# Rank-one attention on one Trainium2 core: argument products over 32 rows, selections built a stage earlier, last averages moved behind the stage boundary

## The reference

```python
def _L3_conv_ref(x, g_w, g_b, theta_w, theta_b, phi_w, phi_b, W_w, W_b, bn_gamma, ...):
    x_avg = jnp.mean(x, axis=(2, 3), keepdims=True)
    se_mid = jax.nn.relu(conv1x1(x_avg, se1_w, se1_b))
    W_cw = jax.nn.sigmoid(conv1x1(se_mid, se2_w, se2_b))
    g_x = conv1x1(x, g_w, g_b).reshape(b, N)
    theta_x = conv1x1(x, theta_w, theta_b).reshape(b, N)
    phi_x = conv1x1(x, phi_w, phi_b).reshape(b, N)
    f = theta_x[:, :, None] * phi_x[:, None, :]
    f_div_C = jax.nn.softmax(f, axis=-1)
    y = jnp.einsum('bij,bj->bi', f_div_C, g_x)
    W_y = conv1x1(y, W_w, W_b)
    W_y = (W_y - bn_mean) * inv + bn_beta
    return W_cw * W_y + x
```

## Time and profile before

| | |
|---|---|
| time, median of 3 runs | 2866.69 us (2864.36 to 2867.64) |
| time of the profiled execution | 2868.04 us |
| its span in the trace | 2866.2 us |
| PE busy | 2743.7 us (96%) |
| DVE busy | 2156.5 us (75%) |
| ACT busy | 1663.3 us (58%) |
| POOL busy | 74.1 us (3%) |
| mean granted PE clock | 0.976 |

### The profile page before, as it was taken

The page is one execution under the profiler, slowest core; times in us unless marked ns, Lnnn a source line. Parts: engine busy times, 40 slices in busy tenths (PEclk is TensorE's granted clock), DMA queues, the critical chain, the costliest instruction groups (busy, mean ns, idle before and its releaser), DMA issues. The chain is left out here.

```text
span 2866.2 us, 45891 instructions
## 1 busy us (share of the span) xinstructions
PE 2743.7 (96%) x20113; PEld 1361.1 (47%) x20113; DVE 2156.5 (75%) x1392; ACT 1663.3 (58%) x2577; POOL 74.1 (3%) x66
## 2 busy tenths in 40 slices
PE   7399999999999999999999999999799999999898
PEld 3334444444344344443444444444478888757552
DVE  5499999999999999999999999998442221224344
ACT  2467776777777777777677777766422222211253
POOL 0000000000000000000000000000431000000000
PEclk9799999999999999999999999999899999999997
DMA  1100000000001000000000000100600000200001
GB/s 69 39 25 22 23 29 9 29 29 16 29 9 35 23 15 29 22 23 29 9 29 29 16 29 10 35 5 1 194 1 0 1 1 0 84 0 1 0 1 59
DMA packets 38760, 72.26 MB, mean 25 GB/s; under 512 B 21088, under 2 KB 22048, under 8 KB 36896
## 3 DMA queue, kind: packets, MB, share of 16 engines
q1 hardware_dynamic: 38496, 69.19, 7.4%
q0 software_dynamic: 64, 0.13, 0.0%
HBM read 60.45 MB, written 8.86 MB: 24 GB/s over the span
## 5 line engine op out<-in xcount | busy, mean ns | idle before, releaser
L734 PE MATMUL l_ps<-mlp_w,W2H 128*64 128x512 f16 x8192 | 1366.4, 392 | 18.0 <-DVE mlp_w L768 18.0
L768 DVE TENSOR_TENSOR mlp_w<-words_x,words_y 128x2048 f32<-128x2048 f32 x512 | 1159.5, 2287 | 66.9 <-PE l_ps L734 66.9
L734 PE MATMUL l_ps<-mlp_w,W2L 128*64 128x512 f16 x4096 | 802.3, 388 | 0.0
L734 PEld LDWEIGHTS l_ps<-mlp_w,W2H 128*64 128x64 f16 x8192 | 455.1, 108 | 550.1 <-issue 116.4
L815 ACT ACTIVATE relu_bottom<-l_ps 128x512 f32<-128x512 f32 x1024 | 612.3, 598 | 79.4 <-PE l_ps L734 1.4
L815 ACT ACTIVATE mlp_w<-l_ps 128x512 f32<-128x512 f32 x684 | 408.8, 598 | 279.7 <-PE l_ps L734 249.8
L752 DVE SCALAR_TENSOR_TENSOR mlp_w<-relu_bottom,sign_ratio,mlp_w 128x2048 f32<-128x2048 f32 x171 | 401.4, 2348 | 7.6 <-ACT relu_bottom L815 7.6
L734 PEld LDWEIGHTS l_ps<-mlp_w,W2L 128*64 128x64 f16 x4096 | 229.0, 109 | 179.7 <-issue 0.8
L815 ACT ACTIVATE relu_top<-l_ps 128x512 f32<-128x512 f32 x340 | 203.2, 598 | 135.7 <-PE l_ps L734 120.8
L723 PE MATMUL l_ps<-y_rows,y_weights_halves 12*128 12x512 bf16 x2048 | 202.4, 385 | 12.5 <-DMA y_rows<-y_pieces 12.5
L752 DVE SCALAR_TENSOR_TENSOR relu_top<-relu_bottom,sign_ratio,relu_top 128x2048 f32<-128x2048 f32 x85 | 199.5, 2348 | 4.0 <-ACT relu_bottom L815 4.0
(11 more groups left out here) (375 smaller groups left out, 2549.3 us busy)
## 6 DMA issues: line engine op xcount, KB each, us to landing
table_pos<-pos_table SPq DMA_DIRECT2D x64, 512.0 KB, 3.8
mlp_w<-in_mlp_w SPq DMA_DIRECT2D x8, 1024.0 KB, 13.2
X<-in_x SPq DMA_DIRECT2D x8, 512.0 KB, 7.4
bias_scratch<-bias_rows SPq DMA_DIRECT2D x64, 64.0 KB, 2.0
mlp_w_hi<-bias_scratch SPq DMA_DIRECT2D x16, 256.0 KB, 3.9
out<-Q SPq DMA_DIRECT2D x16, 256.0 KB, 2.1
y_rows<-y_pieces SPq DMA_DIRECT2D x192, 12.0 KB
xn_b<-in_out_wT SPq DMA_DIRECT2D x1, 1024.0 KB, 7.9
```

Source lines behind the costliest of these rows:

```text
L734: last = nc.tensor.matmul(out[q][a * DH:(a + 1) * DH, :], w[:, half], h[a][:, :, k], start=False, stop=stop, tile_position=(0, a * DH))
L768: nc.vector.tensor_tensor(hw[i % 3][:, r].rearrange("p (m j) -> p m j", j=J), words_x, words_y[:, 2 * n + r].unsqueeze(1).to_broadcast([P, ...
```

## The change

1. `gw`, `sel_q`, `sel_k`, `sel_m` become tiles of the stage before, and POOL's block that fills them moves there, followed by a wait of POOL for its own work. PE's wait for `sel` and DVE's wait for the zeroed `gw` in the rank-one stage go.
2. An argument product takes all 32 rows of its row tile in place of the first 2. The 30 further rows hold zeros in both operands, so the result is the same.
3. `weigh` waits once for both exponentials of its round, ahead of its four products, in place of once per pair.
4. `columns(0)` and `replicate(0, 0)` stand ahead of the weighing of their round, and `replicate(0, 1)` ahead of the last weighing.
5. The last four averages (t = 1) move from the end of ACT's stream in the non-local stage to the head of its stream in the rank-one stage; DVE waits for them (`av_in`) before it adds the halves.

```diff
@@ stage_nonlocal @@
+    K.sel_q, K.sel_k, K.sel_m, K.gw = room([P, B, P]), room([P, B, P]), room([P, B * NT, P]), room([P, CC, 32])
...
+        @block.gpsimd
+        def _(pool):
+            nc.gpsimd.memset(K.gw, 0.0).then_inc(sel, 1)
+            nc.gpsimd.memset(K.sel_q, 0.0).then_inc(sel, 1)
+            nc.gpsimd.memset(K.sel_k, 0.0).then_inc(sel, 1)
+            pool.wait_ge(sel, 3)
...
+            pool.wait_ge(sel, 3 + 4 * B * NT)
...
-            for i in range(NT * CC):
-                t, c = divmod(i, CC)
-                act.wait_ge(o_out, (B - 1) * NT * CC + i + 1)
-                act.wait_ge(mean, CC + i)
-                nc.scalar.activation(ex[2][:, 0:BANK], K.X[:, c, B - 1, t * BANK:(t + 1) * BANK], ACT.Copy,
-                                     accum_out=(K.av_b[:, c:c + 1] if t else K.av[:, c, 1:2])).then_inc(mean, 1)
+            for c in range(CC):
+                act.wait_ge(o_out, (B - 1) * NT * CC + c + 1)
+                act.wait_ge(mean, CC + c)
+                nc.scalar.activation(ex[2][:, 0:BANK], K.X[:, c, B - 1, 0:BANK], ACT.Copy, accum_out=K.av[:, c, 1:2]).then_inc(mean, 1)
@@ stage_rank_one @@
-            pe.wait_ge(sel, 3 + 4 * B * NT)
...
-                        last = nc.tensor.matmul(args[k % 3][:, u], keys[b][at:at + 2, jj * P:(jj + 1) * P], queries[b][at:at + 2, :],
+                        last = nc.tensor.matmul(args[k % 3][:, u], keys[b][at:at + 32, jj * P:(jj + 1) * P], queries[b][at:at + 32, :],
                                                 start=True, stop=True, tile_position=(at, 0))
...
+                pe.wait_ge(ex, NT * (r + 1))
                 for t in range(NT):
                     k = NT * r + t
-                    pe.wait_ge(ex, k + 1)
...
             for r in range(B * JJ):
                 arguments(r)
-                if r:
-                    weigh(r - 1)
                 if r == JJ + 1:
                     columns(0)
                 if r == JJ + 2:
                     replicate(0, 0)
+                if r:
+                    weigh(r - 1)
+            replicate(0, 1)
             weigh(B * JJ - 1)
-            replicate(0, 1)
             columns(1)
...
-            dve.wait_ge(sel, 1)
             nc.vector.tensor_copy(gw[:, :, 0:3], K.v("gtp_w", 0, 3 * CC).rearrange("p (c k) -> p c k", k=3)).then_inc(w_pad, 1)
+            dve.wait_ge(av_in, CC)
             nc.vector.tensor_tensor(av[:, :, 1], av[:, :, 1], K.av_b[:], ALU.add).then_inc(head, 1)
...
+            for c in range(CC):
+                if c:
+                    act.wait_ge(av_in, c)
+                nc.scalar.activation(scaled[1], K.X[:, c, B - 1, BANK:], ACT.Copy, accum_out=K.av_b[:, c:c + 1]).then_inc(av_in, 1)
             act.wait_ge(head, 3)
             act.wait_ge(g_mm, 1)
```

More of the change, by code:

```diff
@@ L1415, in stage_nonlocal @@
     z_mm, z_out, o_mm, o_out = K.sem("z_mm"), K.sem("z_out"), K.sem("nlo_mm"), K.sem("nlo_out")
-    bn, mean = K.sem("bn3_step"), K.sem("mean_sums")
+    bn, mean, sel = K.sem("bn3_step"), K.sem("mean_sums"), K.sem("selection")
     NF = 2 * B
@@ L1422, in stage_nonlocal @@
     with nc.Block() as block:
+        @block.gpsimd
[4 more added lines that the diff above has]
+            pool.wait_ge(sel, 3)
+            for b in range(B):
+                q, k = (w[:, b].rearrange("p (t u r) -> p t u r", t=NT, u=2) for w in (K.sel_q, K.sel_k))
+                for t in range(NT):
+                    n = 32 * (NT * b + t)
+                    nc.gpsimd.tensor_copy(q[:, t, :, 0:2], K.k("ident", n + 1, 1).unsqueeze(2).to_broadcast([P, 2, 2])).then_inc(sel, 1)
+                    nc.gpsimd.tensor_copy(k[:, :, t, 0], K.k("ident", n + 2, 1).to_broadcast([P, NT])).then_inc(sel, 1)
+                    nc.gpsimd.tensor_copy(k[:, :, t, 1], K.k("ident", 3, 1).to_broadcast([P, NT])).then_inc(sel, 1)
+            for n in range(B * NT):
+                nc.gpsimd.tensor_copy(K.sel_m[:, n], K.k("ident", 32 * n + 2, 1).to_broadcast([P, P])).then_inc(sel, 1)
+            pool.wait_ge(sel, 3 + 4 * B * NT)
         @block.tensor
@@ L1621, in stage_rank_one @@
     sums = [room([P, BANK]) for _ in range(B)]
-    sel_q, sel_k, sel_m = room([P, B, P]), room([P, B, P]), room([P, B * NT, P])
+    sel_q, sel_k, sel_m, gw = K.sel_q, K.sel_k, K.sel_m, K.gw
     out = carver(K.Q)([P, CC * B, HW])
-    gw = sb("gtp_w32", [P, CC, 32])
     mid, gate = sb("se_mid", [SE, B]), sb("gate", [P, CC, B])
@@ L1633, in stage_rank_one @@
     pps = args[1][:, 0, 0:2 * B * NT]
-    sel, w_pad, head = K.sem("selection"), K.sem("gtp_w_padded"), K.sem("r1_small")
+    w_pad, head, av_in = K.sem("gtp_w_padded"), K.sem("r1_small"), K.sem("avg_last")
     av_d, g_mm, g_out, t_mm, t_out = K.sem("avg_done"), K.sem("gtp_mm"), K.sem("gtp_out"), K.sem("rowsT_mm"), K.sem("rowsT_out")
@@ L1656, in _ @@
             sp.wait_ge(o_st, 16 * B * NT * CC)
[L1658 to L1672, removed]
         @block.tensor
```

## The result

| | before | changed |
|---|---|---|
| median, first comparison | 2865.53 us (4 runs, 2863.12 to 2867.64) | 2845.95 us (4 runs, 2845.16 to 2847.20) |
| ratio, 95% interval | | 0.9932 [0.9915, 0.9950] |
| profiled execution, span | 2868.04 us, 2866.2 | 2847.20 us, 2845.4 |
| mean granted PE clock | 0.976 | 0.983 |

The account below looks back on a forecast made before the run. PE, at half clock through 27.20 fully busy us of the rank-one loop, was taken as the bound. Handoff 1.0 us plus a shorter loop and tail made 15.4; 2866.69 - 15.4 = 2851.3 us, range 2848 to 2858.5.

Parts of the forecast that it names:

- Clock and rows: Rank-one loop: 2-row argument products let PE's clock fall to 0.50; 32-row ones hold 1.00, at 1.08 us a round.
- rivals 1 and 2: Rank-one loop: 1, clock stays low, 2863.8 us, chance 0.09; 2, clock up for half the rounds, 2858.9 us, 0.07.
- rival 3: Argument products: 32-row products no longer run side by side, 6.9 us at the low clock; about 2902 us, chance 0.04.
- Handoff: Boundary before the rank-one stage: 0.76 us less from the averages, 0.24 from POOL's moved memset, together 1.0 us.
- rival 4: Start of the rank-one stage: averages outlast their 0.3 us of cover, giving 0.8 back: 2852.1 us; inside the 0.80 case.
- Loop and tail: Rank-one stage: first argument products at 2818.77, 14.38 us to replicate(0, 0), then 9.76 led by DVE; last eight outputs at 2842.9.
- Weighing: Rank-one loop: 0.93 us a round at the high clock, five rounds or 4.65 us before replicate(0, 0).
- the later waits for exponentials: Rank-one loop, rounds 3 and 5: PE waits for the exponential three tiles back, 0.24 us each.
- One sign: Rank-one loop: ACT, not PE, stands at the end of most waits if the forecast is right.
- The one wait: Weighing rounds: four products start together, 0.93 us at the high clock; the price is a late start for the first pair.
- The sum: Whole change: last eight outputs start at 2842.9 in place of 2858.26, 15.4 us less, 1.0 of it from the handoff.

Follow-up runs that it names:

- rows32: The kernel before with argument products on 32 rows and nothing else changed: 2850.05 us, ratio 0.9959 [0.9946, 0.9971].
- fill_one: The changed kernel plus seven unused products at the end of PE's stream in the linear stage: 2843.30 us, ratio to the kernel before 0.9931.

## Why the prediction was wrong

The mechanism was right, and the sum of the changed part nearly so. Point by point:

- *Clock and rows:* right. High clock throughout the loop, 32-row products at 1.07 us a round (1.08 taken). The clock of 1.00 excludes rivals 1 and 2 and the 1.07 us rival 3; rows32 shows that the rows alone do it. The Trainium skill's rule (TensorE: Matmul & The Clock Gate, What's actually happening) that the gate follows how busy PE is would fit the 1.00 in the new loop (19.53 of 19.80 us busy), but not the 0.50 at 27.20 of 27.20.
- *Handoff:* 1.0 forecast, 1.01 in the profiles. From the first projection to the first argument product it is 10.1 us in both, so the four averages were ready in time and rival 4 falls.
- *Loop and tail:* from the first argument product to the last eight outputs 24.1 us forecast, 24.45 measured (2812.98 to 2837.43). Weighing was 0.07 us a round too short in the sum, the later waits for exponentials 0.08 too long. Sixteen exponentials took 18.6 us (2814.11 to 2832.71), 18 to 19 forecast. One sign did not come: ACT was to end most waits in the loop, but the chain there lies on PE but for 1.03 us of ACT. The sum's own terms say so, with 2.01 us of PE a round (1.08 + 0.93) against 1.94 of ACT. The one wait had no price and no worth.
- *The sum:* 15.4 forecast, 15.05 in the changed part of the two profiles.
- *The step that failed* is the last one of the sum, "The forecast is for the median: 2866.69 - 15.4", and with it the range, whose lower end allowed only "a run 1.2 below the median". It took the level of three runs for that of the kernel, and took for granted that what the change does not touch takes the same time in both. Neither holds. 63 later runs of the kernel before have medians of 2861.1 to 2863.8 and lie between 2858.1 and 2867.6. From 2862.2 the same 15.4 us give 2846.8; the three medians measured are 2844.6 to 2847.4.
- *What varies* is the place and length of PE's low stretches around idle gaps. Before the rank-one stage six profiles of unchanged early code reach the projection between 2800.3 and 2809.4. In the first pair this gave 5.8 us to the changed kernel, 5.2 of it by the start of the non-local stage. Of these 5.2 us 2.8 arise at one place, after a gap of 3.1 us, in products that are the same in both kernels:

```profile
2487.63 9.97 PE L1232 MATMUL lin_ps<-consts_sb,X 128*128 128x128 f32 x64 [3.09 <-PEq L1049]
```

```profile
2485.28 7.21 PE L1232 MATMUL lin_ps<-consts_sb,X 128*128 128x128 f32 x64 [3.09 <-PEq L1049]
```

  The first is the kernel before, where the granted clock is 0.50 from 2486.5 to 2493.3; in the changed kernel it stays at 1.00. Of the other 2.4 us, 1.3 arise between 2021 and 2095, where the kernel before is at 0.50 for 3.4 us more, and 1.1 ahead of 2021, with no cause shown. For the non-local stage fill_one shows by experiment that it is the clock at those gaps; for the 5 us ahead of it this was not tried.
- Still open is whether the 1 to 2 us by which the later comparisons exceed 15.4 are chance or the shorter boundary's doing (the low stretch at the boundary, seen in one of six profiles with the old handoff and in none of eight with the new one). The intervals of the two comparisons, some 3.6 us to each side, include 15.4.

## What to carry to other kernels

Look at the granted clock beside the busy share: PE can be fully busy and still run at half speed, and here products on 2 of 32 rows did that to everything around them, while zeros in the other rows cost nothing and gave 12 us back. Where PE idles at a stage boundary, unused products in the gap are worth trying; here the median fell by 4.1 us, with intervals that overlap. And before a forecast is set on a few runs' median, ask how far the unchanged part alone moves between executions: a range that leaves this out fails even where the sum is good, as here.

## What was not expected of the hardware

- Sixteen of 32 rows held the clock as well as 32 did, in the one profile taken and by the mean granted clock of all six runs.
- Seven unused products of 0.86 us in one gap took away a low stretch 110 us later as well, in that profile. Whether they did it or chance did, the run does not say.
- The same kernel reaches the same instruction up to 8 us apart in two executions (2801.48 and 2809.41).
